# A two-layer attention and expert kernel: biases folded into weights, bank copies on ScalarE, softmax sums on TensorE, and expert items spread over other rows

## The reference

```python
# 1. causal attention, 16 heads of 8, over the 512 tokens of a batch row
q, k, v = split(x @ W_qkv); att = softmax(causal(q @ k.T * scale)); y = (att @ v) @ W_proj
# 2. experts: 8 experts, the 2 best gates of each token weigh them
h = relu(x @ W1[e] + b1[e]); y = mean_e((h @ W2[e] + b2[e]) * mask[e])      # 128 -> 512 -> 128
# 3. attention of every token over the 16 batch rows at its position, 16 heads of 8
q, k, v = x @ Wq + bq, x @ Wk + bk, x @ Wv + bv
l = q @ k.T * scale; pos = reversed_cumsum(sigmoid(l)); y = softmax(l + cope(q, pos)) @ v @ Wo + bo
# 4. per feature: 128 -> 64, each feature through 16 hidden relu units, 64 -> 128
```

## Time and profile before

| what | value |
|---|---|
| median of 3 runs | 2877.85 us |
| the profiled execution, its own time | 2876.87 us |
| its span | 2875.1 us |
| first half: first exp to last exp | 89.65 to 1240.07 us of the span |
| second half: four steps without attention | to 1389.47 us |
| second half: 17 steps with attention | to the end |
| busy, PE / DVE / ACT / POOL | 79% / 64% / 39% / 27% |
| mean granted TensorE clock | 0.855 of 2.4 GHz |

### The profile page before, as it was taken

How to read it: one execution, slowest core, us unless ns; L and a number is a source line. 1 busy time by engine, 2 the same in 40 slices (tenths; PEclk the granted TensorE clock), 3 DMA queues, 4 the chain that set the end, 5 groups by cost and what they waited for, 6 DMA issues and landing times. The chain is left out here.

```text
span 2875.1 us, 39464 instructions
## 1 busy us (share of the span) xinstructions
PE 2264.1 (79%) x13325; PEld 1312.7 (46%) x13325; DVE 1831.3 (64%) x3363; ACT 1116.0 (39%) x2437; POOL 777.5 (27%) x1430
## 2 busy tenths in 40 slices
PE   3788888999999999989887778777787868633443
PEld 1233223455544545456665556555555656422222
DVE  3455555545555454411487887888778877788984
ACT  0234444555555555544323333433343433322122
POOL 3223333333333333332212123221321232211010
PEclk7677777999999999989988989888888989766666
DMA  5322223222222222000000000000000000000000
GB/s 137 74 58 46 52 50 75 61 59 46 56 70 46 61 60 66 11 18 38 20 30 34 5 13 22 34 16 19 4 34 34 16 19 4 4 4 0 4 4 8
DMA packets 87819, 101.30 MB, mean 35 GB/s; under 512 B 11065, under 2 KB 82369, under 8 KB 83521
## 3 DMA queue, kind: packets, MB, share of 16 engines
q1 hardware_dynamic: 80770, 94.42, 13.4%
q10 hardware_dynamic: 6848, 4.36, 0.6%
HBM read 68.35 MB, written 29.62 MB: 34 GB/s over the span
## 5 line engine op out<-in xcount | busy, mean ns | idle before, releaser
L754 DVE TENSOR_REDUCE maxima<-scores 128x2 f32<-128x1024 f32 (+3 forms) x512 | 421.5, 823 | 559.7 <-PE scores L627 559.5
L860 ACT ACTIVATE probs<-turned 128x512 f32<-128x512 f32 (+3 forms) x1024 | 392.2, 437 | 337.6 <-issue 214.8
L471 PEld LDWEIGHTS rest_bank<-w,hidden 128*128 128x128 f32 x2816 | 392.2, 203 | 171.4 <-issue 164.2
L453 PE MATMUL rest_bank<-xe,w 128*128 128x512 f32 x704 | 391.6, 645 | 64.9 <-ACT hidden L459 49.6
L948 POOL TENSOR_SCALAR_AFFINE_SELECT probs<-probs 128x256 f32<-128x256 f32 x512 | 208.6, 408 | 687.8 <-ACT probs L860 678.9
L471 PE MATMUL rest_bank<-w,hidden 128*128 128x128 f32 x2816 | 394.6, 287 | 0.0
L459 ACT ACTIVATE hidden<-rest_bank 128x512 f32<-128x512 f32 x352 | 208.1, 595 | 471.8 <-PE rest_bank L453 331.8
L1648 POOL TENSOR_SCALAR shift<-mv2b 128x4 f32<-128x4 f32 x48 | 11.9, 247 | 940.4 <-DVE mv2b L1375 940.4
L624 PE MATMUL scores<-k_stack,q_stack 48*128 48x512 bf16 (+3 forms) x1024 | 181.9, 332 | 62.1 <-DVE maxima L754 53.9
L645 PE MATMUL turned<-q_stack,k_stack 51*128 51x512 bf16 (+3 forms) x1024 | 196.7, 329 | 31.1 <-ACT probs L860 15.4
L656 PE MATMUL o_bank<-probs,v_ext 128*32 128x512 f32 (+3 forms) x2048 | 217.1, 499 | 0.5 <-ACT outs L867 0.3
(11 more groups left out here) (232 smaller groups left out, 3444.6 us busy)
## 6 DMA issues: line engine op xcount, KB each, us to landing
mask_all<-mask_scratch SPq DMA_DIRECT2D x32, 1024.0 KB, 5.0
stack_q<-parts_q SPq DMA_DIRECT2D x96, 128.0 KB, 2.4
stack_k<-parts_k SPq DMA_DIRECT2D x96, 128.0 KB, 2.4
q_stack<-stack_q SPq DMA_DIRECT2D x32, 384.0 KB, 6.3
k_stack<-stack_k SPq DMA_DIRECT2D x32, 384.0 KB, 9.4
x<-in_L_attn_batch_dram SPq DMA_DIRECT2D x16, 256.0 KB, 5.4
w<-in_L_ffn_W_dram ACTq DMA_DIRECT2D x16, 256.0 KB, 3.0
out_dram<-x SPq DMA_DIRECT2D x16, 256.0 KB, 2.3
```

Source lines behind the costliest of these rows:

```text
L453: pe.matmul(bank[:, :], t.w1[:, x % E, f * P:(f + 1) * P], m.xe[:, x % XE, :], start=True, stop=True).then_inc(m.s_h, 1)
L471: mm = pe.matmul(bank[:, n * P:(n + 1) * P], m.hidden[:, q % 4, n * P:(n + 1) * P], t.w2[:, k, :], start=False, stop=(k == E * F - 1), ski ...
L754: dve.tensor_reduce(mx[:, w % 2, :, p, qt], s_bank[:, :, 0:(qt + 1) * P], AX.X, ALU.max)\
L860: act.activation(probs[:, 2 * p + e, KEYS_AT[kt]:KEYS_AT[kt] + width], st_bank[:, e, 0:width], ACT.Exp, scale=SCALE).then_inc(s_exp, 1)
```

## The change

Seven things change together.

1. The biases of the queries, keys, values and kink heights are folded into the weights, as is already done for the experts' first layer: a normalised row sums to zero, so with 1 added to each of its elements a row of column sums carries the bias. PE computes the column sums and DVE adds them to the weights, in row 2 of the first half. The copy into `kept` adds the 1.
2. ACT instead of DVE takes keys and values (k = 9, 10), queries (k = 4) and kink heights (k = 5, 7, 10, 15) out of the banks. The output bias b_o is added by PE, with four matmuls of one row of ones, and statistics and scaling of the projection read the bank itself.
3. The softmax weights are summed by PE: 16 accumulating matmuls of the identity with 64 columns each, at k = 1.
4. `HALVED = ()`: the second mix has 16 transposes, and DVE's half add goes.
5. In `v_step` the statistics of the expert sum, or else of the keys, come before the weight sums.
6. In the first half both products of an item stand in the same even step: the output product of the item before, then the hidden product of this one.
7. Items start at row 3, step 24, not at row 5: `EARLY = 6` (192 items). The first four groups are now batch rows 0 to 3. Seven groups have their gates in the first half, not six. 12 further items stand in the tail of the first half, between the last turn and projection. The second half begins with three steps of 20, 16 and 16 items, not four of 16, and of the steps with attention i = 0 to 9 have 24 items, i = 10 has 16, and the rest none.

```diff
-EARLY = 5
+ROWS_FIRST = 4
+EARLY = 6
+TAIL_ITEMS = 12
-FIRST_ITEM_STEP = 32 * 5 + 24
-GATES_IN_ROW = {5: 0, 6: 1, 9: 2, 10: 3, 13: 4, 14: 5}
+FIRST_ITEM_STEP = 32 * 3 + 24
+GATES_IN_ROW = {3: 0, 4: 1, 6: 2, 8: 3, 10: 4, 13: 5, 14: 6}
...
+    def pe_attention_columns(pe, n, bank):
+
+        weights, biases = ((t.w_at, t.b_at), (t.w_kink, t.b_kink))[n]
+        width = (3 * D, 2 * NPOS * H)[n]
+        pe.wait_ge(m.s_biased, E + n)
+        pe.matmul(bank[:, 0:width], minus_mean, weights[:, :], start=True, stop=False)
+        pe.matmul(bank[:, 0:width], plus_mean, biases[0:1, :], start=False, stop=True).then_inc(m.s_columns, 1)
...
-                    before, item = item_at(*step_before(b, w, s)), item_at(b, w, s)
-                    if before is not None and before < EARLY_ITEMS:
-                        m.pe_expert(pe, before, y_bank)
+                    if b == 2 and w == 0 and s in (0, 4):
+                        m.pe_attention_columns(pe, s // 4, h_bank)
+                    item = item_at(b, w, s)
+                    if item is not None and 0 < item <= EARLY_ITEMS:
+                        m.pe_expert(pe, item - 1, y_bank)
                     if item is not None and item < EARLY_ITEMS:
                         m.pe_hidden(pe, item, h_bank, item)
...
                 pe_values(pe, S - 1, 1, QUADS - 1, 3)
+                pe_tail_items(pe, 0, 2)
                 pe_turn_outputs(pe, S - 1, 3, fill_no(S - 1, "last_turn3"))
-                for piece in range(2):
-                    pe_project_out(pe, piece, fill_no(S - 1, f"last_out{piece}"))
+                pe_tail_items(pe, 2, 4)
+                pe_project_out(pe, 0, fill_no(S - 1, "last_out0"))
+                pe_tail_items(pe, 4, 6)
+                pe_project_out(pe, 1, fill_no(S - 1, "last_out1"))
+                pe_tail_items(pe, 6, TAIL_ITEMS)
+                m.pe_expert(pe, EARLY_ITEMS + TAIL_ITEMS - 1, y_bank)
...
-HALVED = (1,)
+HALVED = ()
...
+        def pe_weight_sums(pe, i):
+            pe.wait_ge(s_p, i)
+            for k in range(S):
+                mm = pe.matmul(w_bank[:, 0:G * H], t.ident[:, :], acc[:, k, :, :].rearrange("p g h -> p (g h)"),
+                               start=(k == 0), stop=(k == S - 1))
+            mm.then_inc(s_wsum, 1)
...
-                mm = pe.matmul(m2[:, j * P:(j + 1) * P], o_t[:, j * P:(j + 1) * P], t.w_o[:, :], start=True, stop=True)
+                pe.matmul(m2[:, j * P:(j + 1) * P], o_t[:, j * P:(j + 1) * P], t.w_o[:, :], start=True, stop=False)
+                mm = pe.matmul(m2[:, j * P:(j + 1) * P], m.ones_row[:, :], t.b_o[0:1, :], start=False, stop=True)
...
+                    if k == 1:
+                        pe_weight_sums(pe, i)
...
-            dve.wait_ge(s_p, i)
-            own(dve.tensor_reduce(wsum[:, :], by_key(acc), AX.X, ALU.add))
-            dve.wait_ge(s_vec_q, own.value())
-            own(dve.reciprocal(wsum[:, :], wsum[:, :]))
+            dve.wait_ge(s_wsum, i)
+            own(dve.reciprocal(wsum[:, :], w_bank[:, 0:G * H]))
...
             dve.wait_ge(s_m2, n2 + 2)
-            dve.tensor_tensor(y2[:, :, :], m2[:, :].rearrange("p (g d) -> p g d", g=G),
-                              t.b_o[:, :].unsqueeze(1).broadcast_to([P, G, D]), ALU.add).then_inc(s_m2_read, 1)
-            dve.wait_ge(s_m2_read, n2 + 3)
-            v_stats2(dve, own, i, 1, lambda j: y2[:, j, :])
+            v_stats2(dve, own, i, 1, lambda j: m2[:, j * P:(j + 1) * P])
...
+            if step.summed is not None:
+                m.v_sum_stats(dve, step.summed)
+            elif keys is not None:
+                v_keys_stats(dve, keys)
             if finish:
                 v_weight_sums(dve, own_q, i)
-            if step.summed is not None:
-                m.v_sum_stats(dve, step.summed)
...
-            if attend:
-                v_queries(dve, i)
...
+                if k in (9, 10) and keys is not None:
+                    a_keys_values(act, keys, k - 9)
+                if k == 4 and attend:
+                    a_queries(act, i)
+                if k in (5, 7, 10, 15) and attend:
+                    a_kink_heights(act, i, (5, 7, 10, 15).index(k))
```

134 lines of the change are left out of this document (73 added, 61 removed).

## The result

The changed kernel takes 2864.61 us (median of 8 runs, 2856.3 to 2872.17); the kernel before, run beside it, 2877.82 us (8 runs, 2863.72 to 2879.99). The ratio is 0.9957, with a 95% interval of 0.9941 to 0.9973: 12 us faster, where 69 were forecast. The time lies outside the range (2750 to 2852). The profiled execution after takes 2860.1 us, its span is 2858.4 us; both are read against 2876.87 and 2875.1 us of before.

A forecast was written before the change was run, and what follows sets the result against it. PE bounds first-half rows with items; in the second half no engine is full, though DVE leads. First half +22.3, tail -9.5 and second half -82 sum to -69, giving 2808 us; range 2750 to 2852.

The forecast's parts named there:

- Up to logits 0: Second half, last add to logits 0: eight steps with a sum start 3.8 us earlier (best 7, worst 0.3), -30.
- Both small chains finding such a gap after each multiply: Steps with a sum: POOL's sum and keys operations fit between DVE's multiplies; the -30 assumed this.
- a rival at 0.10: Steps with a sum: DVE's multiplies shut out POOL's chains, two more operations blocked 2.3 us each, +37: 2845; chance 0.10.
- Plain steps: Steps with items but no sum (i = 5, 9), up to logits 0: net -1.3 us each, -2.6 together.
- +1.2 twice (i = 4, 8): Steps i = 4 and 8: DVE waits for ACT's copy of the total at k = 1, +1.2 us each.
- Weight sums: PE's sums take 3.5 us (7 low), hidden with items, saving 2.7 on PE; exposed in i = 1, +5.7.
- low level at step borders: Rival: TensorE stays at the low clock where steps meet, +65, 2873, no change; chance 0.06.
- The tail and the short steps, -9.5: End of first half and short steps: 12 items use PE's 8.7 us to spare, one short step goes; -5 to -12.
- Pairing, +9: First half, both products in one step: idle time gained against 2.4 us of waits a row; -11 to +29, middle +9.
- odd steps: Rival: first-half odd steps without an item stay as long as in itemless rows, +150 instead of +9: 2949; chance 0.06.
- stand under DVE's logits: Second half: the four b_o matmuls, 0.9 us, are covered by DVE's logits.
- Behind logits 0: Second half, after logits 0: b_o's add and two kink adds leave DVE, -1.75 us a step, -30 in all.

The follow-up runs named there:

- roots_dve: Changed kernel with the small chains of sum and keys on DVE, not POOL, a reciprocal replacing the root: 2830.5 us, 0.9827 of before.
- kv_both: Changed kernel with ACT copying both halves of keys and values ahead of the relu of item 9: 2848.8 us, 0.9905 of before.
- stats_late: Changed kernel with DVE's statistics of the sum moved back behind the reciprocal, its multiply and the weighted values: 2878.3 us, 1.0005 of before.
- yield_port: Changed kernel with two added DVE waits for POOL's small chains, behind the statistics of the sum and of the keys: 2839.7 us, 0.9874 of before.
- sums_dve: Changed kernel with softmax weights summed by one DVE reduce, PE's sixteen matmuls left out: 2849.9 us, 0.9912 of before.
- no_bo: Changed kernel without the four one-row matmuls adding b_o, so that bias is left out: 2857.0 us, 0.9916 of before.
- best2: Changed kernel with DVE waiting for POOL's chains, both key/value copies before the relu, group 7's gates earlier, DVE weight sums at i = 1, 4, 8: 2803.8 us.

## Why the prediction was wrong, and where it was right

**"Up to logits 0", the steps with a sum, -30.** This is the step that failed with the largest consequence. Steps i = 2 to 10 were to be 45 us shorter and are 12.5 longer. The forecast had logits 0 follow the sum's chain one for one. The first half of that is right: in i = 6 the keys' chain on POOL ends 16.5 us after the last add, 2.1 earlier than before (18.6), and PE's transposes of the keys' rows start at 18.4 us and not at 22.2 (where they stood in PE's own queue and did not wait for rows): the 3.8 of the sum. But from there to logits 0 it takes 11.1 us, where it took 6.7, so logits 0 stay (29.5 for 28.9; my worst case was 0.3 earlier). The timelines of PE and DVE of the kernel before, i = 6, last add at 1929.4:

```profile
1946.33 2.07 PE L1279 MATMUL rest_bank<-w_kink,kept 128*128 128x512 f32 x2 [5.02 <-DVE kinks L1395]
...
1951.54 0.60 PE L1259 MATMUL rest_bank<-ident,xn 128*128 128x128 f32 x4
1951.98 1.04 PE L1288 MATMUL rest_bank<-ident,prod 128*128 128x128 f32 x8
...
1958.27 2.29 DVE L1403 TENSOR_TENSOR prod<-q,kv 128x2048 f32<-128x2048 f32 x1
```

Against the same places of the changed kernel (L1301, L1337 and L1438 in the timeline of roots_dve's section), 0.8 us are the eight more transposes of mixture 1, 1.7 their low level, 0.4 that of the keys' transposes, and 1.3 the copy on ACT behind the relu. The forecast had the first and the last of these at 0.9 and 0.6 in the plain steps and at nothing in the steps with a sum; kv_both shows the copy alone to be worth 1.5 us at logits 0. PE's 5 us of idle time are not new. Before, they lay ahead of a kink product, and the low level fell on the products ahead of the transposes; now they lie right ahead of the transposes, and it falls on mixture 1. stats_late confirms that the earlier place of the statistics is worth nothing in i = 2, 3, 6 and 7.

**"Both small chains finding such a gap after each multiply".** This is the second half of the same failure. I had the 3.13 us of the earlier trace rows in hand and took it as a rival at 0.10, against it "after the sum's statistics comes a reciprocal, which let POOL through before". Before, that reciprocal stood ahead of the statistics and the multiply followed them, so the chain was shut out there already (6.3 us), and in the changed kernel the reciprocal is 0.5 us long. The adds that left DVE were what POOL slipped between: the keys' chain of steps with a sum grew from 2.3 to 3.5 or 4.1 us. yield_port shows what it costs: with the chain free PE keeps the high level, logits 0 of i = 2, 3, 6 and 7 come at 25.9, and i = 2 to 10 are 24.5 us shorter (kv_both gives 18.9 there and sums_dve 20.9; the three overlap). That 25.9 lies so near the 25.5 that I had forecast is partly luck, as the copy's detour is still in it. The rival's price, +37, was for two operations; its time, 2845, was closer than mine.

**"Plain steps", -1.3.** The terms that stand there (-2.7, -1.5, +0.9 and +0.6) add up to -2.7 and not to -1.3. Measured at logits 0: +0.9. The transposes come 1.2 us earlier (15.1 for 16.3), and the way from there to logits 0 is 2.0 us longer, all of it at the high level.

**"+1.2 twice (i = 4, 8)".** Mis-sized by a factor of five or more: these steps grew by 7.2 and 7.9 us, and sums_dve gives 6.7 and 6.2 of it back. I counted ACT's copy at k = 1 as it stood, 4.1 us after the last add, and not that PE's weight sums stand at k = 1 ahead of it, at the low rate. The 7 us at the low level were in the text; what I missed is who is queued behind them.

**Weight sums.** Size and place were right elsewhere: 3.7 to 3.8 us in i = 2, 3, 6 and 7, over before the last add, 7.1 in the steps without items, and PE starts warm. i = 1 grew by 7.4 us for 5.7. In i = 5 and 9, the plain steps, PE waits 1.2 and 1.6 us for the exp, the sums run partly at the low rate (5.6 and 6.0 us), end behind the last add, and the two hidden products after them take 3.5 and 3.1 us for 2.1: there is no warm start to gain, and these steps are at 90.5 and 89.6 us where I said 86. The rival "low level at step borders" held in these two and in i = 4 and 8, and in no other step with items but i = 1, where no last add stands.

**The tail and the short steps, -9.5.** The time given back there is named: 9.9 us by the mask of group 7, computed in the short step right ahead of its items. I moved group and items in my sum, but looked at no chain between them. The tail itself is worth 3.3.

**Pairing, +9.** Wrong in sign. I added up 2.4 us of new waits a row, relu and exp at the start of odd steps; none of it showed. PE's idle time went, as in my lower bound, and its busy time fell by 1.5 us a row in addition. The rival "odd steps" is dead: row 5 takes 70.90. The error of some 20 us worked against the others, so that the total of the kernel hides how far off the sum was behind the first half.

**The four b_o matmuls "stand under DVE's logits".** Not all of them: DVE waits 20.5 us for the projection, 5.4 without b_o, and no_bo takes 9.6 us off, 3.2 of it in i = 16, which the forecast had 1.75 us shorter and which is 3.3 us longer (58.5 for 55.2).

**"Behind logits 0", -1.75 a step.** Right where there are no items: from logits 0 to the last add, i = 13, 14 and 15 are 1.7 us shorter each. In i = 2 to 9 it is between 2.3 shorter and 1.0 longer, 0.9 shorter on average.

**Right:** rows 3 and 4 (74.5 on average in eleven profiles, and 73.6, for 75.6 and 74.1); steps i = 13 to 15 (71.6 to 72.2 us for 73); the items that leave, in i = 11 and 12; PE as the busiest engine of a step with items, near 80 us (80.1 and 84.2). That best2 comes to 2804 us, near the 2808 of the forecast, does not prove the sum: it has edits that I had not counted on, and its stretch behind the first half is 1559 us where the forecast comes to 1631.6 - 92 = 1540. The two totals meet because the first half is better than forecast.

**Open:** why rows with both products in one step have less busy time on PE; how much of what plain steps i = 5 and 9 lack is the sums (sums_dve gives 1.4 and 2.2 us back there); what mixture 1 would cost with DVE's half add put back (`HALVED = (1,)`), which no run has; how yield_port's gain is shared between its two waits; and whether b_o in one wider matmul would cost less, which was not tried.

## What to carry to other kernels

When work leaves an engine, list who used its gaps: here POOL's chain of four tiny operations ran between DVE's reads of banks, and without them it set when the keys' rows came, how long PE stood idle ahead of them, and by that PE's clock. A wait on the engine that has time to spare can be an optimisation: two waits of 2.4 us on DVE gave 3.6 us at logits 0. When a chain gets earlier, also follow what stands between its end and the goal: here 3.8 us were won at the transposes and 4.4 lost behind them. And of an operation put into another engine's queue, ask at every position in the loop what stands behind it there: the weight sums ahead of one copy cost 13 us in two steps.

## What the runs showed of the hardware

- DVE's multiply holds up POOL's operations even when these have 4 elements a partition: 0.23, 1.04 and 0.20 us became 1.29, 2.95 and 1.19. While DVE waited, they took 0.23, 1.04 and 0.20 again. It works the other way too: the multiply that started 0.09 us behind a POOL operation of 1.26 us took 3.33 us for 2.29 (yield_port). The Trainium skill (SBUF — State Buffer, section "SBUF: two separate sides") says that a DVE operation with two SBUF inputs and a GpSimd operation that reads SBUF exclude each other for the whole instruction; these rows agree.
- Eight short matmuls in a row, four of them with a single row of b_o, left PE's clock at the low level with no idle time in the 10 us ahead of it (i = 5): the hidden product behind them took 2.08 us, and 1.02 without the b_o matmuls. In other steps (i = 6 and 9 of the changed kernel, 1.12 us) the same eight were followed by one near the high rate, so they do not always do it.
- One batch row of the same code took from 71.1 to 78.8 us in different executions, with the granted clock of the early slices between 0.5 and 0.9; from row 5 on the executions mostly agree. A gain of 10 us in a later stretch is invisible in the median of five runs, and plain in the stretch.
